# First attention: GpSimd computes the third polynomial step of nine of ten root tiles

## What is computed

```python
cos = einsum('bhsd,bhtd->bhst', l2norm(q), l2norm(k))     # 16 heads, 2048 x 2048
g_dist = arccos(clip(cos, -1 + 1e-7, 1 - 1e-7))
attn_score = (1.0 + g_dist) ** (-3.2)
n_r, n_c = attn_score.sum(-1), attn_score.sum(-2)
k_tilde = attn_score / n_r[..., :, None] / n_c[..., None, :]
probs = k_tilde / maximum(k_tilde.sum(-1, keepdims=True), 1e-12)
out = einsum('bhst,bhtd->bhsd', probs, v)
```

## Time and profile before

| | us |
|---|---|
| median of 3 runs (3964.8 to 3969.72) | 3966.16 |
| the profiled execution | 3964.4 |
| its span | 3962.6 |
| busy over the span: TensorE (matmul) | 3159.4 (80%) |
| busy: VectorE | 2984.2 (75%) |
| busy: ScalarE | 3180.3 (80%) |
| busy: GpSimd | 1175.7 (30%) |

### The profile page before, as it was taken

The page is one execution under the profiler, slowest core; times in us unless marked ns, Lnnn a source line. Parts: engine busy times, 40 slices in busy tenths (PEclk is TensorE's granted clock), DMA queues, the critical chain, the costliest instruction groups (busy, mean ns, idle before and its releaser), DMA issues. The chain is left out here.

```text
span 3962.6 us, 59670 instructions
## 1 busy us (share of the span) xinstructions
PE 3159.4 (80%) x18880; PEld 1315.8 (33%) x18880; DVE 2984.2 (75%) x4684; ACT 3180.3 (80%) x2658; POOL 1175.7 (30%) x746
## 2 busy tenths in 40 slices
PE   4777787778777877787777575888888888888899
PEld 2221122112211221122111232355555555555547
DVE  6777977797779777977797798878787787788411
ACT  2699999999999999999998564488788787888822
POOL 2111011101110111011100043477677676777700
PEclk8776677667766776677667698799999999999999
DMA  1000000000000000000000135011001000110000
GB/s 38 32 7 7 0 6 6 6 0 6 6 6 2 5 6 6 4 3 6 6 5 5 35 124 154 22 39 28 23 23 44 23 23 23 39 28 23 18 19 11
DMA packets 59591, 86.13 MB, mean 22 GB/s; under 512 B 9808, under 2 KB 45904, under 8 KB 58960
## 3 DMA queue, kind: packets, MB, share of 16 engines
q1 hardware_dynamic: 59344, 83.06, 7.4%
HBM read 52.44 MB, written 30.54 MB: 21 GB/s over the span
## 5 line engine op out<-in xcount | busy, mean ns | idle before, releaser
L1089 POOL TENSOR_TENSOR lo<-pr,hi 128x1024 f16<-128x1024 f32 x384 | 916.7, 2412 | 396.9 <-ACT hi L1215 394.8
L1138 DVE TENSOR_REDUCE mx<-mx_ps 128x1 f32<-128x512 f32 x1024 | 660.1, 684 | 175.1 <-PE mx_ps L1253 171.8
L660 PE MATMUL r_ps<-qst,kst 72*128 72x512 bf16 x1024 | 575.6, 565 | 252.2 <-DVE wt L470 188.9
L1230 ACT ACTIVATE pr<-s_ps 128x1024 f32<-128x1024 f32 x512 | 531.6, 1038 | 275.4 <-PE s_ps L1274 243.8
L664 PE MATMUL r_ps<-mst 110*128 110x512 f16 (+1 forms) x1024 | 512.7, 507 | 81.5 <-DVE wt L451 35.4
L1215 ACT ACTIVATE hi<-pr 128x1024 f16<-128x1024 f32 x512 | 547.3, 1070 | 0.0
L287 POOL COPY mono_x<-two 128x256 f32 (+1 forms) x16 | 8.5, 530 | 1781.4 <-PE t_ps L633 1727.9
L1253 PE MATMUL mx_ps<-ka,qa 128*128 128x512 f16 x1024 | 385.3, 397 | 139.3 <-DVE mx L1138 116.4
L589 ACT ACTIVATE wt<-wt 128x2048 f32<-128x2048 f32 x256 | 484.6, 1895 | 0.0
L580 ACT ACTIVATE wt<-wt,theta_bias 128x8192 f32<-128x8192 f32 x64 | 453.6, 7111 | 0.2
L1293 PE MATMUL pv_ps<-vh,hi 128*128 128x129 f16 x4096 | 434.2, 223 | 11.3 <-ACT sums L1221 5.8
(11 more groups left out here) (179 smaller groups left out, 4302.6 us busy)
## 6 DMA issues: line engine op xcount, KB each, us to landing
qk<-stg SPq DMA_DIRECT2D x6, 2048.0 KB, 13.6
vh<-v SPq DMA_DIRECT2D x16, 520.0 KB, 3.6
qa<-qk SPq DMA_DIRECT2D x16, 512.0 KB, 3.7
ka<-qk SPq DMA_DIRECT2D x32, 256.0 KB, 4.8
v<-v_st SPq DMA_DIRECT2D x3, 2080.0 KB, 7.9
qst<-parts_dram SPq DMA_DIRECT2D x144, 32.0 KB
kst<-parts_dram SPq DMA_DIRECT2D x144, 32.0 KB
qk<-stg SPq DMA_DIRECT2D x4, 1024.0 KB, 8.3
```

The source lines that it names most:

```text
L660: mm = eng.matmul(r_ps[:, r % 2, :], kst[:, cols(k)], qst[:, cols(n_, BANK)], start=True, stop=True)
L1089: eng.tensor_tensor(lo[:, i % NHL, :, :], pr_slot(i), hi[:, i % NHL, :, :], ALU.subtract).then_inc(lo_done, 1)
L1138: eng.tensor_reduce(mx4[:, q // NCH, q % NCH:q % NCH + 1], mx_ps[:, q % 2, :], AX.X, ALU.max)\
L1230: eng.activation(pr_slot(i), s_ps[:, i % 2, :, :], ACT.Exp, scale=SM).then_inc(exp_done, 1)
```

## The change

- Root tiles become ten, log tiles six (`NL = 6`). The groups of `theta` are cut at 0, 6, 10, 13, 15, 16.
- Step 3 of root tiles 0 to 8 moves to GpSimd (`shift_and_multiply`), which has no instruction for add-and-multiply here and takes two `tensor_tensor` of 128 x 1,024 for each half: subtract a constant (broadcast from one column), multiply. Tile 9 keeps step 3 on VectorE (`multiplied`, signalled by `own`). Step 2 writes to `two` and a new buffer `vb` in turn.
- VectorE's queue takes step 4 of a tile (`closed`) two tiles after its steps 1 and 2 (`raised`, `folded`). `folded(j)` waits until GpSimd is done with tile j-2, whose buffer it writes.
- The first 44 ring chunks stay 512 wide in two slots. All later ones are 1,024 wide in three slots: the two of `m_ps`, free once the squares are read, and the pair of banks of `r_ps`. The last two chunks (tile 9's step 4) stand behind the `stack` copies.
- `ring_to` is worked out anew, with GpSimd's half at `PRODUCT_US` = 4.8.
- TensorE weighs only one tile of the previous head in the new head, behind its fourth square instead of ahead of its third. `turn_factors` goes through `m_ps` in two pieces, `stack` copies them with two instructions. The previous head's `finish` stands behind tile 1's step 2, its `finish_rows` behind tile 1's step 4.
- GpSimd builds the monomials two heads ahead, in two parts (`products`, `factors`). Its loop over heads is unrolled.
- The reciprocals of `values` go through PSUM (`rc_ps`), with a copy. `attn0` shares the memory of `v0`.

The diff, cut to its core:

```diff
-NL = 8
+NL = 6
...
+    RA = 4
+    GROUPS = (0, NL, NL + 4, NL + 7, NT - 1, NT)
...
+    narrow = [(0, RAISE), (0, FOLD), (1, RAISE), (1, FOLD)]
+    for j in range(2, RA):
+        narrow += [(j, RAISE), (j, FOLD), (j - 2, CLOSE)]
+    narrow += [(RA, RAISE)]
+    wide = [(RA, FOLD)] + [(NQ + j, CLOSE) for j in range(NL)] + [(RA - 2, CLOSE)]
+    for j in range(RA + 1, NQ):
+        wide += [(j, RAISE), (j, FOLD), (j - 2, CLOSE)]
+    wide += [(NQ - 2, CLOSE), (NQ - 1, CLOSE)]
...
-    ROOT_US, CHUNK_US, HALF_US = 1.035, 0.69, 1.24
...
+    ROOT_US, CHUNK_US, PRODUCT_US, LOAD_US, LAG_US = 0.954, 0.625, 4.8, 1.3, 1.5
...
+        def slot(r):
+            if r < R1:
+                return r_ps[:, r % 2, :]
+            q = (r - R1) % 3 if r < RE else (2, 0)[r - RE]
+            return m_ps[:, q, :] if q < 2 else pair_ps
...
+                def shift_and_multiply(h, j):
+
+                    at = v_at(j)
+                    half = 2 * BANK // width(at)
+                    for i in range(2):
+                        v = folds(j, i, 2 * BANK)
+                        eng.wait_ge(ring_read, NRING * h + at + half * (i + 1))
+                        eng.tensor_tensor(v, v, shift[:, 0:1].to_broadcast([P, 2 * BANK]), ALU.subtract)\
+                           .then_inc(shifted, 1)
+                        eng.wait_ge(shifted, NCU * h + 2 * j + i + 1)
+                        u = wt[:, j, cols(i, 2 * BANK)]
+                        eng.tensor_tensor(u, v, u, ALU.mult).then_inc(cubic, 1)
...
+                for h in range(H):
+                    for j in range(RA + 1):
+                        shift_and_multiply(h, j)
+                    if h + 2 < H:
+                        eng.wait_ge(mono_ready, h + 2)
+                        products(eng, sb, h + 2, mono)
+                    for j in range(RA + 1, NQ - 1):
+                        shift_and_multiply(h, j)
+                    if h + 2 < H:
+                        eng.wait_ge(fac_turned, 2 * h + 4)
+                        factors(eng, sb, h + 2, mono, mono_ready)
...
                 def head(h, first=False, last=False):
+                    for j in range(RA):
+                        raised(h, j)
+                        folded(h, j)
+                        if j >= 2:
+                            closed(h, j - 2)
+                        if j == 1 and not first:
+                            finish(h - 1)
                     if not first:
-                        values(h - 1, NT - 2, 2)
-                    for j in range(QH):
-                        root_tile(h, j)
+                        finish_rows(h - 1)
+                    raised(h, RA)
+                    folded(h, RA)
                     for j in range(NL):
                         log_tile(h, j)
-                    for j in range(QH, NQ):
-                        root_tile(h, j)
...
+                    closed(h, RA - 2)
+                    for j in range(RA + 1, NQ):
+                        raised(h, j)
+                        folded(h, j)
+                        if j == NQ - 1:
+                            multiplied(h, j)
+                        closed(h, j - 2)
                     values(h, 0, GROUPS[1])
+                    closed(h, NQ - 2)
                     if not last:
-                        for j in range(4):
-                            stack(h + 1, j)
+                        for x in range(2):
+                            stack(h + 1, x)
+                    values(h, GROUPS[1], GROUPS[2] - GROUPS[1])
+                    closed(h, NQ - 1)
...
                     theta(h, 0)
-                    theta(h, 1)
-                    for p in range(0, GROUPS[1]):
+                    for p in range(NT):
+                        if p + 1 in GROUPS[1:4]:
+                            theta(h, GROUPS.index(p + 1))
+                        if p == NT - 1:
+                            theta(h, NG - 1)
                         score(h, p)
...
                 def head(h, first=False, last=False):
-                    if not first:
-                        weigh(h - 1, NT - 2)
-                        weigh(h - 1, NT - 1)
                     done = 2
                     for g in range(NM0):
                         if g >= 2:
                             square(h, g)
+                        if g == 3 and not first:
+                            weigh(h - 1, NT - 1)
                         for r in range(done, ring_to[g]):
                             ring(h, r)
```

More of the change, by code:

```diff
@@ L212, in _ @@
                 eng.wait_ge(qkn_ready, 1)
-                monomials(eng, sb, 0, mono, mono_ready)
+                products(eng, sb, 0, mono)
+                factors(eng, sb, 0, mono, mono_ready)
             @block.scalar
@@ L319, in stage_attention0, with width, chunk, u_at @@
     NQ = NT - NL
-    QH = NQ // 2
-    GROUPS = (0, 4, NL, NL + QH, NT)
+    RA = 4
+    GROUPS = (0, NL, NL + 4, NL + 7, NT - 1, NT)
+    NG = len(GROUPS) - 1
     NM0 = 2 * NT
-    NRING = 12 * NQ + 4 * NL
-    NCU = 2 * NQ
+    NCU = 2 * (NQ - 1)
     NSG = NL // 2
-    def q_at(j):
-        return 12 * j if j < QH else 12 * j + 4 * NL
+    RAISE, FOLD, CLOSE = range(3)
+    narrow = [(0, RAISE), (0, FOLD), (1, RAISE), (1, FOLD)]
[6 more added lines that the diff above has]
+    wide += [(NQ - 2, CLOSE), (NQ - 1, CLOSE)]
+    R1 = NCH * len(narrow)
+    NRING = R1 + 2 * len(wide)
+    RE = NRING - 2
+    ring_at = {step: NCH * i for i, step in enumerate(narrow)}
+    ring_at |= {step: R1 + 2 * i for i, step in enumerate(wide)}
+    def width(r):
+        return BANK if r < R1 else 2 * BANK
+    def chunk(r):
+        return (*narrow[r // NCH], r % NCH) if r < R1 else (*wide[(r - R1) // 2], (r - R1) % 2)
+    def u_at(j):
+        return ring_at[j, RAISE]
+    def v_at(j):
+        return ring_at[j, FOLD]
+    def f_at(j):
+        return ring_at[j, CLOSE]
     def s_at(j):
-        return 12 * QH + 4 * j
+        return ring_at[NQ + j, CLOSE]
     def place(tile):
@@ L638, in square @@
                     if g == 0:
-                        eng.wait_ge(mst_ready, 4 * (h + 1))
-                    if not (isinstance(h, int) and h == 0 and g < 2):
+                        eng.wait_ge(mst_ready, 2 * h + 2)
+                        if not (isinstance(h, int) and h == 0):
+                            eng.wait_ge(ring_read, NRING * h)
+                    if g >= 2:
                         eng.wait_ge(m0_read, NM0 * h + g - 1)
@@ L681, in turn @@
                     eng.wait_ge(o_copied, h + 1)
-                    if not (isinstance(h, int) and h == H - 1):
-                        eng.wait_ge(mst_ready, 4 * (h + 2))
                     for j in range(4):
@@ L701, in head @@
                             square(h, g)
+                        if g == 3 and not first:
+                            weigh(h - 1, NT - 1)
                         for r in range(done, ring_to[g]):
                             ring(h, r)
+                            if r == f_at(0) and not first:
+                                turn(h - 1)
                         done = max(done, ring_to[g])
-                    for r in range(done, NRING):
+                    for r in range(done, RE):
                         ring(h, r)
-                    if not first:
-                        turn(h - 1)
-                    for p in range(NL):
+                    for p in range(3):
                         weigh(h, p)
                     if not last:
-                        for j in range(4):
-                            turn_factors(h + 1, j)
-                    for p in range(NL, NL + QH):
+                        for x in range(2):
+                            turn_factors(h + 1, x)
+                    for p in range(3, GROUPS[1]):
+                        weigh(h, p)
+                    ring(h, RE)
+                    ring(h, RE + 1, last)
+                    for p in range(GROUPS[1], GROUPS[2]):
                         weigh(h, p)
@@ L717, in head @@
                         start(h + 1)
-                    for p in range(NL + QH, NT - 2):
+                    for p in range(GROUPS[2], NT - 1):
                         weigh(h, p)
@@ L723, in _ @@
                 eng.wait_ge(const_ready, 1)
-                for j in range(4):
-                    turn_factors(0, j)
+                for x in range(2):
+                    turn_factors(0, x)
                 start(0)
```

238 lines of the change are left out of this document (127 added, 111 removed).

## The result

The changed kernel takes **3814.27 us** (median of four runs, 3811.62 to 3816.82) where the kernel before takes 3965.48 on the same chip: a ratio of 0.9617, 95% interval 0.96 to 0.9634, or 151 less. The forecast was 3767, with a range of 3735 to 3832. The direction and the two largest terms (ScalarE's work and its waits before arctangents) held; the waits before the logarithms did not, and the time came out 47 above, outside the forecast's own 3735 to 3794 and inside the range only by the part that was added for two rivals. The profiled execution took 3812.16, its span is 3810.4.

A forecast was written before the change was run, and what follows sets the result against it. ScalarE's work plus its waits was taken to bound the attention: 115.6 + 3.0 + 0.1 + 0.2 = 118.9 a head. 199.5 off 3964.4 gave 3764.9, plus 1.8 for the median: 3767 us, range 3735 to 3832.

The forecast's parts named there:

- ScalarE's work: ScalarE's busy time per head: 122.5 less 7.0 for two log tiles, plus 0.1 for a fifth theta, gives 115.6.
- Arctangent waits: ScalarE's waits for VectorE's cosine products before arctangents: 4.0 a head go, 0.1 is kept.
- GpSimd's pace: P, GpSimd's time for a half of step 3: 4.4, from two operations at the median; just in time for VectorE.
- rival at the mean: GpSimd's half takes 4.9, so tile 1 is done 2.0 late once per head: 3799, chance 0.13.
- GpSimd as the bound: GpSimd busy throughout decides the head from P = 5.1; at P = 6.3 the program takes about 4140; chance 0.03.
- Cover at the end of the head: Tile 8's step 4 ends at 97.7 after the head's first root, ScalarE asks for it at 104.0: 6.3 to spare.
- The wait for the third square: At a head's start, one weighing of 0.9 behind the fourth square: ScalarE waits 0.8 instead of 3.25.
- cold-clock rival: TensorE's low clock in the root stage makes narrow chunks 0.69 instead of 0.605, 3.7 a head: 3827, chance 0.13.
- VectorE up to the last logarithm: VectorE's narrow chunks and previous head's output end at 31.9, level with ScalarE's roots and logarithms; chunk 43 adds 0.2.
- Less comes off: Rival: waits created by the order, such as squares behind ring chunks on TensorE's queue, eat half: 3866, chance 0.08.
- The sum: The first attention: 118.9 a head, 12.5 less, over fifteen heads 187.5, plus 12.0 in the first head: 199.5 less.
- The signs: What the trace would show if right (table loads 118 to 120 apart, ScalarE 97% busy) or wrong (slow products, idle ScalarE).

The follow-up runs named there:

- e1: The changed kernel with the previous head's `finish_rows` moved behind step 1 of tile 4: 3755.64 us.
- e2: The changed kernel with the small maximum in `finish_rows` taken in PSUM instead of SBUF: 3798.25 us.
- e4: The changed kernel with the ring plan's time for GpSimd's half, `PRODUCT_US`, at 4.3 instead of 4.8: 3804.12 us.
- e10_warm: Edits of e1 and e2, last weighing behind the eighth square (3754.05 us), plus 14 zero-weight matmuls ending each head but the last: 3728.78 us.
- e12: e10_warm with step 3 of all tiles on VectorE and the ring plan adapted: 3919.09 us.

## Why the prediction came out as it did

- **ScalarE's work** 122.5 to 115.6: measured 115.65, and the exchange undone costs 7.1 a head. Right.
- **Arctangent waits** 4.0 to 0.1: measured 0.0. Right, and so were the wide chunks at 1.135 (two in 2.35).
- **GpSimd's pace**, P = 4.4 from the median of a float16 operation: measured 4.27 to 4.34 in the third head. The parts differ from what the row suggested: the subtraction, whose second input is a broadcast column, takes 1894 ns and the multiplication 2392. The rival at the mean (4.9) and the one of GpSimd as the bound both fall. The Trainium skill's figure (GPSIMD Engine Reference, section 3.1) gave 4.6 as an estimate; the measurement is below it. That GpSimd has no instruction for add-and-multiply, as the section on the change has it, no run here shows; none tried one.
- **Cover at the end of the head**: tile 8's step 4 ends at 466.5, 103.0 after the first root at 363.46, and theta asks for it at 472.21, 108.75 after. Forecast 97.7 and 104.0: both late by the same 5, the cover is 5.7 instead of 6.3. `multiplied` took 6.01 where I had up to 4.2.
- **The wait for the third square**, where I took one weighing at 3.64/4 = 0.9: wrong. That row was measured at clock 1.00. With one weighing left and not two, and `values` in between, TensorE idles 3.75 ahead of the head's third square, and the weighing takes 1.73. My cold-clock rival had the mechanism, but put it at VectorE's pace through all narrow chunks, where the clock is 1.00. The wait came at 1.61 + 0.21 instead of 0.8 (its largest part is 1.6 to 2.7 over the heads), and ring chunk 2 reached VectorE at 5.05 instead of 3.9.
- **"VectorE up to the last logarithm ... level", which "adds 0.2"**: the step that failed. Chunk 2 is late by 1.15, the plan's waits for step 4 (its half is 4.8 long) cost 1.8 in this head (0.41 + 0.94 + 0.23 + 0.23), `finish_rows` takes 3.64 instead of 2.0, and the chunks came every 0.63 where I had 0.605, 1.1 in 42. "Level" became 5 to 6 late, and squares behind chunks 42 and 43 turned this into 4.34 + 0.26 for ScalarE. I had the queue order in view and gave it 0.2, though "level" left no slack for any error; the `LAG_US` and `PRODUCT_US` in the plan were read as settings, not as waits. e1 shows that 63 of 64.6 hang on where `finish_rows` stands, e2 that about 24 are the one slow instruction, e4 that 12.6 are the plan's.
- **"Less comes off"** named this mechanism in a clause, at 3866 and a chance of 0.08. It was the right rival, mis-sized at half the gain.
- **The sum.** Heads 1 to 15: 1791.9 forecast (1978.90 - 12.0 - 14 x 12.5), 1851.9 measured: 60.0 of the 61 that the attention's sum missed. The first of them, which has no previous output to finish and no weighing ahead of it, took 121.9, 5.4 under its forecast of 127.3; the other fourteen took 123.6 each, 4.7 over 118.9. The 14 that brought the time back towards the forecast come from the second attention, and no step of mine claims them: that is luck. So is the range: 3832 was chosen for GpSimd at the mean, which did not happen, and for a low clock through all narrow chunks, where it was 1.00; the mechanism that cost the time had 3866 beside it, outside the range.
- **The signs.** ScalarE's busy share of a head is 94%, not 97%, and the table loads lie 123 apart, not 118 to 120; GpSimd's busy time, 88.7, and the arctangents came as written. The products took 1.89 and 2.39, not 2.1 to 2.2, and `multiplied` 6.01. Of the signs of being wrong one came in part, 3.5 a head idle before roots, at a clock of 0.72 over the third head's start; none named a wait before the logarithms, where most of the time went.

What stays open: why the second attention's length moves between 1224.6 and 1237.0, and the 1.7 a head still idle before roots in e10_warm (0.68, 0.50 and less).

## What to carry to other kernels

When a forecast says that two engines arrive "level", price the order in which they queue behind each other: a wait then costs its full length, and moving 3.6 of side work by one step (e1) was worth more than a third of what the whole change brought. An instruction row taken from a stretch at one clock is no price for the same instruction after a gap; look at what the engine did before it. Filling TensorE's idle gap pays only while the gap is there (e10 against e12), so a change of any other engine's end must be checked against it.
